# A decoder layer on one core: the last weighted sum moved to the end of its own step, and GpSimd's element operations cut into blocks of 256 columns

## The reference

```
x = layernorm(x + attn(x))    # damped complex recurrence over the 32 sequences, state' = c*state + x;
                              # real part of the state, times x
x = layernorm(x + xattn(x, ctx))   # 16 heads of 16 channels, relu projections, softmax, own layer norm
x = layernorm(x + ffn(x))     # each token goes to the nearest of 8 experts, a*silu(g), fp32
```

## Time and profile before

| what | before |
|---|---|
| median of 3 runs | 1257.54 us (1252.96 to 1257.8) |
| the profiled execution's own time | 1257.0 us |
| its span | 1255.2 us |
| mean granted TensorE clock | 0.935 |
| PE busy | 1119.9 us (89%) |
| DVE busy | 942.7 us (75%) |
| ACT busy | 669.9 us (53%) |
| POOL busy | 783.9 us (62%) |

### The profile page before, as it was taken

The page is one execution under the profiler, slowest core; times in us unless marked ns, Lnnn a source line. Parts: engine busy times, 40 slices in busy tenths (PEclk is TensorE's granted clock), DMA queues, the critical chain, the costliest instruction groups (busy, mean ns, idle before and its releaser), DMA issues.

```text
span 1255.2 us, 27516 instructions
## 1 busy us (share of the span) xinstructions
PE 1119.9 (89%) x8060; PEld 820.0 (65%) x8061; DVE 942.7 (75%) x2416; ACT 669.9 (53%) x1416; POOL 783.9 (62%) x932
## 2 busy tenths in 40 slices
PE   3799989999999998989999999752999999999996
PEld 2466666666666666656666666431888888888885
DVE  7558998988988998999898898763555555555553
ACT  4166776766667776767676777641222222222221
POOL 4637888888878988879888865561233333333333
PEclk9689999999989999999999999555999999999998
DMA  4676676665555565556556555042111111111110
GB/s 131 146 179 194 174 207 183 182 156 139 141 140 146 149 158 137 147 139 161 136 146 156 136 134 126 11 151 59 44 51 47 43 50 50 49 47 48 50 51 22
DMA packets 90826, 144.91 MB, mean 115 GB/s; under 512 B 12663, under 2 KB 78336, under 8 KB 84513
## 3 DMA queue, kind: packets, MB, share of 16 engines
q1 hardware_dynamic: 83616, 126.09, 38.6%
q0 software_dynamic: 6528, 16.99, 4.6%
q10 hardware_dynamic: 576, 0.53, 0.2%
HBM read 91.44 MB, written 53.03 MB: 115 GB/s over the span
## 4 chain that ended last, share of the span: by engine, by line
PE 45%; DVE 19%; POOL 15%; issue 10%; DMA 8%; SPq 2%; ACT 1%; POOLq 0%; DVEq 0%; ACTq 0%
PE Y L454 10%; PE G L422 8%; PE A L422 8%; DVE neg_max_sb L1243 7%; PE S L1004 3%; PE M L988 3%; DMA k_st<-k_pieces 3%; DMA k_pieces<-k_lo 3%; DVE oq L1370 3%; POOL buckets L802 2%; PE GT L432 2%; PE O L980 2%; POOL rs L729 2%; POOL by_re L694 2%; PE M L960 2%
## 5 line engine op out<-in xcount | busy, mean ns | idle before, releaser
L1243 DVE TENSOR_REDUCE neg_max_sb<-S 128x2 f32<-128x512 f32 x512 | 328.3, 682 | 71.0 <-PE S L1004 69.2
L864 ACT ACTIVATE probs<-T 128x512 f32<-128x512 f32 x512 | 277.9, 595 | 148.1 <-PE T L1017 136.8
L1004 PE MATMUL S<-k_st,q_st 48*128 48x256 f32 x1024 | 215.3, 321 | 46.3 <-DMA k_st<-k_pieces 27.8
L1004 PEld LDWEIGHTS S<-k_st,q_st 48*128 48x128 f32 x1024 | 147.3, 194 | 123.7 <-issue 53.5
L1017 PE MATMUL T<-q_st,k_st 49*128 49x256 f32 x1024 | 211.9, 321 | 9.8 <-ACT probs L864 8.1
L1017 PEld LDWEIGHTS T<-q_st,k_st 49*128 49x128 f32 x1024 | 148.0, 195 | 28.3 <-ACT probs L864 17.0
L399 ACT ACTIVATE gT<-GT 128x512 f32<-128x512 f32 x71 | 42.5, 599 | 209.4 <-PE GT L432 209.4
L980 PE MATMUL O<-probs,v_aug 128*32 128x256 f32 x2048 | 151.0, 416 | 0.7 <-ACT probs L864 0.7
L378 POOL DMA_INDIRECT out<-res,token x71 | 76.4, 1077 | 103.3 <-DVE res L499 98.8
L454 PE MATMUL Y<-dn_sb,gT 128*128 x568 | 134.2, 379 | 0.8 <-ACT gT L399 0.8
L802 POOL DMA_INDIRECT buckets<-row,slot x64 | 69.7, 1089 | 85.0 <-DVE slot L1425 74.8
(11 more groups left out here) (184 smaller groups left out, 2541.1 us busy)
## 6 DMA issues: line engine op xcount, KB each, us to landing
q_st<-q_pieces SPq DMA_DIRECT2D x64, 256.0 KB
k_st<-k_pieces SPq DMA_DIRECT2D x64, 256.0 KB
xr<-buckets SPq DMA_DIRECT2D x71, 129.0 KB, 2.1
xt<-in_x SPq DMA_DIRECT2D x32, 256.0 KB, 6.3
ct<-in_ctx SPq DMA_DIRECT2D x32, 256.0 KB, 6.8
q_pieces<-q_hi SPq DMA_DIRECT2D x32, 256.0 KB, 2.1
q_pieces<-q_lo SPq DMA_DIRECT2D x32, 256.0 KB, 2.2
q_st<-q_pieces SPq DMA_DIRECT2D x64, 128.0 KB
```

The source lines that it names most:

```text
L864: a_.activation(probs[:, h % 8].rearrange("p k t -> p (k t)"), T_ps[h % 2][:, :], ACT.Exp, scale=DH ** -0.5).then_inc(s["exp_ok"], 1)
L1004: last = t_.matmul(S_ps[h % 2][:, c * TOK:(c + 1) * TOK], q_st[base:base + STACK, h, c * P:(c + 1) * P], k_st[base:base + STACK, h, :], st ...
L1243: v.tensor_reduce(neg_max[:, cur.mod(2), :, h], S_ps[h % 2][:, :].rearrange("p (c t) -> p c t", c=NTC), AX.X, ALU.max, negate=True).then_i ...
```

## The change

Two edits. PE's `weighted_sum` of the last four heads is called at head 15 of the step in which the other three groups are summed, behind the flip of `ct`, instead of at head 1 of the next step, and ACT's copy of the sums moves from head 2 to head 0. GpSimd's element operations in the steps are written as loops over the two token blocks (and the two factors), so that each instruction has 256 columns; only the last of a loop raises the semaphore. The products become four instructions, the eight operations of 512 columns become two each.

```diff
-                both = [P, 2, NTC, C]
-                re_b = decay_re.unsqueeze(1).to_broadcast([P, NTC, C])
-                pair_b = decay[:, :, :].unsqueeze(2).to_broadcast(both)
-
@@ conv_products
-                    g.tensor_tensor(by_re[:, :, :, :], state[:, 0].unsqueeze(1).to_broadcast(both), pair_b, ALU.mult).then_inc(s["conv"], 1)
+                    for w in range(2):
+                        for c in range(NTC):
+                            last = g.tensor_tensor(by_re[:, w, c], state[:, 0, c], decay[:, w], ALU.mult)
+                    last.then_inc(s["conv"], 1)
@@ conv_real (conv_imag and conv_input likewise)
-                    g.tensor_tensor(state[:, 0], by_re[:, 1], state[:, 1], ALU.subtract).then_inc(s["conv"], 1)
+                    for c in range(NTC):
+                        last = g.tensor_tensor(state[:, 0, c], by_re[:, 1, c], state[:, 1, c], ALU.subtract)
+                    last.then_inc(s["conv"], 1)
@@ weigh
-                    g.tensor_tensor(xw[:, :, :], row[:, item.mod(2), :, 0:C], scale_bc[:, :].unsqueeze(1).to_broadcast([P, NTC, C]),
-                                    ALU.mult).then_inc(s["xw_ok"], 1)
+                    for c in range(NTC):
+                        last = g.tensor_tensor(xw[:, c], row[:, item.mod(2), c, 0:C], scale_bc[:, :], ALU.mult)
+                    last.then_inc(s["xw_ok"], 1)
@@ cut
-                    g.tensor_tensor(lo[:, :, :], src, hi[:, :, :].bitcast(F32), ALU.subtract).then_inc(s[done], 1)
+                    for c in range(NCH):
+                        last = g.tensor_tensor(lo[:, c], src[:, c], hi[:, c].bitcast(F32), ALU.subtract)
+                    last.then_inc(s[done], 1)
@@ step of GpSimd
-                        g.tensor_tensor(x1[:, a.mod(4)], x1[:, a.mod(4)], b_bc[:, :].unsqueeze(1).to_broadcast([P, NTC, C]),
-                                        ALU.add).then_inc(s["x1b_ok"], 1)
+                        for c in range(NTC):
+                            last = g.tensor_tensor(x1[:, a.mod(4), c], x1[:, a.mod(4), c], b_bc[:, :], ALU.add)
+                        last.then_inc(s["x1b_ok"], 1)
@@ step of ScalarE, h == 0
                                 a_.activation(x1T[:, :, :].rearrange("p o t -> p (o t)"), M_ps[0][:, :], ACT.Copy).then_inc(s["x1T_ok"], 1)
+                            if active(a):
+                                copy_sums(a, 1)
@@ step of ScalarE
-                        if h == 2 and active(a):
-                            copy_sums(a, 1)
@@ step of TensorE, h == 1
-                            if active(a):
-                                weighted_sum(a, 3)
@@ step of TensorE, end
                             flip(M_ps[0], ct[:, nn.mod(2)]).then_inc(s["ctT_pe"], 1)
+                        if h == 15 and active(prv):
+                            weighted_sum(prv, 3)
```

More of the change, by code:

```diff
@@ L709, in conv_imag @@
                         wait(pool, "conv", item, 5, 2)
-                        g.tensor_tensor(state[:, 1], state[:, 1], re_b, ALU.mult).then_inc(s["conv"], 1)
+                        for c in range(NTC):
+                            last = g.tensor_tensor(state[:, 1, c], state[:, 1, c], decay_re, ALU.mult)
+                        last.then_inc(s["conv"], 1)
                     else:
                         wait(pool, "conv", item, 5, 3)
-                        g.tensor_tensor(state[:, 1], state[:, 1], by_re[:, 0], ALU.add).then_inc(s["conv"], 1)
+                        for c in range(NTC):
+                            last = g.tensor_tensor(state[:, 1, c], state[:, 1, c], by_re[:, 0, c], ALU.add)
+                        last.then_inc(s["conv"], 1)
                 def conv_input(item):
@@ L719, in conv_input @@
                     wait(pool, "conv", item, 5, 4)
-                    g.tensor_tensor(state[:, 0], state[:, 0], xt[:, item.mod(2)], ALU.add).then_inc(s["conv"], 1)
+                    for c in range(NTC):
+                        last = g.tensor_tensor(state[:, 0, c], state[:, 0, c], xt[:, item.mod(2), c], ALU.add)
+                    last.then_inc(s["conv"], 1)
                 def rstd(item, ready, per, mv, rs, done):
```

## The result

The change takes 1265.2 us (median of 16 runs, 1259.44 to 1272.31), the kernel before 1254.73 us (median of 16, 1245.2 to 1263.64). The ratio of the comparison is 1.0104 with a 95% interval of 1.0081 to 1.0127: about 13 us slower, where the two medians alone stand 10.5 us apart. The profiled execution took 1267.28 us with a span of 1265.5.

What follows compares the result with a forecast made beforehand. A loop through GpSimd, `dist`, DVE's pick and `slot` bounds the kernel: 13.96 + 10.1 = 24.1 us a step, +0.2. Over 27 steps +5, filling and draining 1 us, on 1257.0: 1263, rounded down to 1262; range 1241 to 1279.

Steps and rivals of the forecast that it cites:

- The loop: Transfers, GpSimd to `dist`, DVE's pick, `slot`, next transfers: said to set each step, 24.1 us against 23.91; chance 0.52.
- The cost of a block: Each added GpSimd instruction was to cost 0.135 us; seven between transfers and `dist` 0.95 us, all on the loop.
- GpSimd's part: Stretch from the indirect transfers to the end of `dist`: 12.91 us, to grow by 0.95 + 0.1 to 13.96.
- From `dist` to the transfers: Second stretch of the step, through DVE's pick and `slot`: 9.22 us without collisions plus 0.9, so 10.1 us.
- the 9.22 us without collisions: One step's 11.15 us from `dist` to the transfers, less the excess of one `oq` and `onehot_bf` at their worst.
- just three operations collide: Behind the pick only two `oq` and one `onehot_bf` were counted as held by GpSimd: excess 0.94 us, then 0.9.
- `u`: DVE operation ahead of the pick: median to fall from 2.51 to near 1.1 us, giving nothing on the loop.
- The moved sum: Weighted sum of the last heads, moved on PE: the second pair of scores was to come 0.7 to 1.5 us earlier.
- held steps: The 8 of 20 steps where `dist` waits for ACT, 10.4 us together; expected to become ordinary steps of 24.1 us.
- B: Rival: blocks let DVE slip in and collisions behind the pick nearly vanish; step 23.4 us, 1243 us; chance 0.23.
- C: Rival: DVE waits at the pick, PE's scores of heads 10 and 11 come late, clock falls; 1270 to 1284 us; 0.18.
- D: Rival: the sum's move gains all 1.07 us on PE, GpSimd's cost hidden; step 22.9 us, 1230 us; chance 0.07.

Runs made afterwards that it cites:

- e3: The kernel before plus seven 16-column additions on GpSimd ahead of the products in every full-pipeline step, cutting nothing; ratio 1.0252.
- e4: The kernel before plus the same seven 16-column additions on GpSimd, placed where it idles waiting for `slot`; ratio 1.005.
- e6: The kernel before plus the moved weighted sum, with only GpSimd's operations ahead of `dist` cut into blocks (seven more instructions a step); ratio 1.0161.
- e5: The kernel before plus the moved weighted sum, with only GpSimd's operations behind `dist` cut into blocks (four more instructions a step); ratio 0.9962.
- e2: The kernel before with only the weighted sum and its copy moved, GpSimd's operations left whole; ratio 1.0008.
- e7: The kernel before plus the moved sum, GpSimd's operations behind `dist` in blocks, and `dist` placed ahead of `q_lo`; ratio 1.003.

## Why the prediction was right, and where it wasn't

The loop. It said that the step is set by transfers, GpSimd, `dist`, pick and `slot`, and that is shown: e3 against e4, and e6 against e5, put equal or similar work on the loop and off it, with 25 us between e3 and e4 and 25 us (1.61% against -0.38%) between e6 and e5.

The cost of a block. 0.135 us was taken; it is 0.13 to 0.15 (1.37 against 1.24 for the bias, 1.38 against 1.23 for `q_lo`), 0.9 to 1.05 us for seven. GpSimd's part grew by 0.99 us to 13.90, where 13.96 was forecast, and the pick is 0.13 behind `dist` as before.

The estimate that the prediction worked out from the Trainium skill's "GPSIMD Engine Reference", section 7 (about 102 cycles for a read command), was 1.19 us for the seven; the part grew by 0.99, so the measurement stands nearer to the 0.95 of the rows.

From `dist` to the transfers: this is the term that was mis-sized, 10.1 us as predicted, 10.40 as measured. Over 27 steps 0.3 us make 8; less the 1.6 that the first part is shorter by, that is about the distance between the forecast of 1257.0 + 5 and the 12 that the steps measure. Two things in it failed.

First, the 9.22 us without collisions. It was worked out from one step with the longest durations of the whole stretch, 1.455 and 1.276 us, but that step had these:

```profile
601.90 1.41 DVE L1370 TENSOR_TENSOR oq<-o,qn 128x256 f32<-128x256 f32 x1
603.25 1.25 DVE L1405 TENSOR_TENSOR onehot_bf<-expert_no,choice 128x16 bf16<-128x16 f32 x1
```

That gives 11.15 - 0.76 - 1.095 = 9.30. The mean of all steps before (10.33 us) less the mean excess of 0.94 gives 9.39, so the term was 0.1 to 0.2 us short before anything was changed.

Second, and this is the step of the prediction that fails, that just three operations collide. Their means after the change:

```profile
L1381 DVE TENSOR_TENSOR oq<-o,qn 128x256 f32<-128x256 f32 x40 | 30.6, 764 | 0.0
...
L1416 DVE TENSOR_TENSOR onehot_bf<-expert_no,choice 128x16 bf16<-128x16 f32 x20 | 11.0, 551 | 0.0
```

The excess did shrink for `oq` (mean 0.76 us, where "near 0.95" was expected), not for `onehot_bf` (0.55): together it is 2 x (0.76 - 0.65) + (0.55 - 0.16) = 0.61 us, less than the 0.9 that were put in. But three others that had been clear of GpSimd, or nearly so, began to meet it. `place`, `o` and `cand` of DVE, before and then after (ns min/median/max, 209 to 689 us):

```profile
L1418 DVE TENSOR_TENSOR place<-place,onehot_bf x20: 165/169/175, 224.6 to 678.8; 128x16 f32<-128x16 f32 x20
...
L1377 DVE SCALAR_TENSOR_TENSOR o<-oq,mvx,g_bc x40: 474/477/485, 224.2 to 678.9; 128x256 f32<-128x256 f32 x40
...
L1395 DVE TENSOR_TENSOR cand<-dist,least x20: 165/224/229, 218.7 to 672.9; 128x16 f32<-128x16 f32 x20
```

```profile
L1429 DVE TENSOR_TENSOR place<-place,onehot_bf x19: 160/167/629, 230.0 to 668.3; 128x16 f32<-128x16 f32 x19
...
L1388 DVE SCALAR_TENSOR_TENSOR o<-oq,mvx,g_bc x38: 470/476/758, 229.5 to 668.3; 128x256 f32<-128x256 f32 x38
...
L1406 DVE TENSOR_TENSOR cand<-dist,least x20: 215/378/441, 223.2 to 685.9; 128x16 f32<-128x16 f32 x20
```

Their means went from 169 to 285 ns, from 477 to 557 (twice a step) and from 199 to 369, which adds 0.45 us a step: 1.06 us of collisions in all, where 0.9 was forecast and 0.94 was there before.

`u`. Its median fell by 1.58 us to 0.93, further than the 1.1 that was forecast, and its mean by 1.05 (1961 to 912 ns). It is worth nothing on the loop, as predicted; the idle time in front of the pick shows it.

The moved sum. That it ends the held steps is right (8 to 1). That these then count as ordinary steps is right in the whole change only because its blocks let `u` through. Alone (e2) the sum uncovers the key projection's wait and TensorE's lower clock (0.94 in the mean of the full pipeline, 0.97 before), which the prediction placed only as a rival's mishap at heads 10 and 11. One sum of its working is off: a sum of 1.07 us behind 635.80 ends at 636.87, not near 636.97, which changes nothing that follows.

Rivals. B, fewer collisions: no, they move from one operation to the next. C, PE late and its clock down: its first half came, DVE's wait at the pick (33.4 us) and with it PE's longer waits for DVE's maxima (20.8 us, 10.2 before), but the clock of the full pipeline stayed at 0.96 against 0.97, and the loop's two parts account for the whole step. D, the waits for keys and scores are what the kernel pays for: no, the waits for keys fell by 9 us and the time rose.

The number. 1265.2 us lies 3 us from the forecast of 1262, but part of that is luck. The forecast was 5 us more than 1257.0; the comparison has 13 more, from a kernel before whose median there was 1254.73. Measured by the prediction's own 0.5% this is "slower", which had 0.37, no more than "same".

## What to carry to other kernels

A long list of short waits can hide a loop that closes once a step; look for two events with a constant distance (here 12.91 us within 0.03, in the twelve steps that weren't held) and for a handover with always the same small latency. An added instruction costs its fixed part on that loop and little beside it, so cut an engine's operations only where its partner is on the loop and it isn't: with the moved sum, blocks behind `dist` and a mere change of order ahead of it gave 1.5%, the blocks everywhere cost 1.0%. Blocks don't end collisions; they make each one shorter and let others happen. And an edit that makes an engine early may gain nothing if it then waits and its clock falls behind the wait.

## What the runs showed of the hardware

In these traces `u` of DVE, with two inputs in SBUF, and an elementwise operation of GpSimd don't run together: `u` ended 0.55 us behind the products of 2.37 us, and against blocks of 0.73 us its longest duration fell from 2533 ns to 968. Its shortest is 680, so it was held for 0.29 us at most, though the four blocks of the products follow one another without a pause. Even an operation of 16 columns pays for it: `onehot_bf` took 1.25 us where 0.16 is its least.

TensorE's clock fell to 0.50 behind a wait of 0.77 us at the key projection in e5, which then took 3.50 us; behind 0.38 us at the same place before the change it took 1.97 us. But in e7 it took 1.96 us behind 0.91 us, so the length of the wait alone doesn't decide.
